# Delta layer: the outer products of the block solve run in pairs on two column tiles, and half of one output projection moves between them

## What is computed

```python
x = _layernorm(x + _L0_attn_ref(...))
...
x = _layernorm(x + _L1_attn_ref(x, w_qkvz, w_ba, conv_w, dt_bias, A_log, norm_weight, w_out))
...
x = _layernorm(x + _L3_ffn_ref(...))
```

## Time and profile before

| | us |
|---|---|
| median of 3 runs | 2424.78 |
| lowest and highest run | 2412.61, 2426.64 |
| span of the profiled execution | 2424.5 |
| PE, DVE, ACT, POOL busy in it | 2112.7, 1856.6, 1477.2, 216.2 |
| the delta layer's rounds 1 to 13, first `upper` to first `upper` | 715.52 |

### The profile page before, as it was taken

One profiled execution on the slowest core, in us unless ns is written; L12 is line 12 of the kernel. 1 busy time (PEld: TensorE's weight loads), 2 busy tenths in 40 slices (PEclk: granted clock), 3 DMA queues, 4 the chain that ended last, 5 costly groups with the idle time before them and its releaser, 6 DMA issues. The chain is left out here.

```text
span 2424.5 us, 42274 instructions
## 1 busy us (share of the span) xinstructions
PE 2112.7 (87%) x16920; PEld 1596.5 (66%) x16920; DVE 1856.6 (77%) x3341; ACT 1477.2 (61%) x2466; POOL 216.2 (9%) x163
## 2 busy tenths in 40 slices
PE   7997447999999999999986589899999996888855
PEld 4666325777777777878774345788888873555633
DVE  4776667888989898889867834478888776678697
ACT  3664255667777777776736631577777775455365
POOL 0000100000100010101100042000000000100313
PEclk8998768999999999999988799999999996999977
DMA  3000012222222221222116355311010000200001
GB/s 159 2 1 12 13 34 53 72 83 57 64 56 66 56 64 54 62 74 80 36 49 212 129 143 176 115 32 57 23 27 6 5 18 1 81 2 1 16 1 35
DMA packets 164785, 135.14 MB, mean 56 GB/s; under 512 B 118512, under 2 KB 145776, under 8 KB 157936
## 3 DMA queue, kind: packets, MB, share of 16 engines
q1 hardware_dynamic: 160752, 126.02, 16.6%
q0 software_dynamic: 3840, 6.43, 1.4%
HBM read 106.42 MB, written 25.98 MB: 55 GB/s over the span
## 5 line engine op out<-in xcount | busy, mean ns | idle before, releaser
L1593 DVE SCALAR_TENSOR_TENSOR ctx_chan<-l1a_raw,l1a_cw,ctx_chan 128x1024 f32<-128x1024 f32 x192 | 232.0, 1279 | 3.5 <-issue 3.5
L1200 PE MATMUL banks<-x_chan,l1a_wp 128*128 128x512 f32 x512 | 225.2, 598 | 4.8 <-ACT l1a_vt L1488 4.8
L1200 PEld LDWEIGHTS banks<-x_chan,l1a_wp 128*128 128x128 f32 x512 | 98.0, 192 | 122.6 <-issue 116.7
L3166 PE MATMUL banks<-x_chan,more_weights_ahead 128*128 128x128 f32 x1024 | 123.6, 275 | 1.2 <-ACT l2a_kT L2693 1.2
L3166 PEld LDWEIGHTS banks<-x_chan,more_weights_ahead 128*128 128x128 f32 x1024 | 121.6, 192 | 3.9 <-ACT l2a_kT L2693 2.0
L1187 POOL TENSOR_TENSOR l1a_al<-l1a_aT,l1a_outer 128x1024 f32<-128x1024 f32 x32 | 75.0, 2364 | 483.2 <-DVE l1a_aT L1653 483.2
L1237 PE MATMUL banks<-l1a_wo,l1a_oT 128*128 128x256 f32 x512 | 117.7, 383 | 0.0
L2706 ACT ACTIVATE l2a_masked<-l2a_masked,l2a_rowmax 128x128 f32<-128x128 f32 x256 | 99.0, 392 | 28.9 <-DVE l2a_rowmax L2919 28.9
L3202 PE MATMUL banks<-l2a_wo,l2a_oT 128*128 128x256 f32 x512 | 114.5, 382 | 0.0
L1208 PE MATMUL banks<-l1a_wz,x_chan 128*128 128x256 f32 x512 | 113.4, 380 | 0.0
L3202 PEld LDWEIGHTS banks<-l2a_wo,l2a_oT 128*128 128x128 f32 x512 | 96.2, 190 | 14.3 <-issue 1.0
(11 more groups left out here) (648 smaller groups left out, 5644.1 us busy)
## 6 DMA issues: line engine op xcount, KB each, us to landing
l1a_sq<-l1a_norm_mem SPq DMA_DIRECT2D x16, 1024.0 KB, 4.7
ctx_tok<-l1a_rows_mem SPq DMA_DIRECT2D x16, 1024.0 KB, 8.1
l1f_wgu<-in_l1f_wgu_dram SPq DMA_DIRECT2D x4, 1408.0 KB, 11.4
moe_sums<-l1x_zero SPq DMA_DIRECT2D x2, 2176.0 KB, 18.3
ctx_chan<-in_ctxT_dram SPq DMA_DIRECT2D x2, 2048.0 KB, 13.8
l1a_wp<-in_l1a_wp_dram SPq DMA_DIRECT2D x8, 512.0 KB, 5.5
l1f_wgu<-moe_sums SPq DMA_DIRECT2D x8, 512.0 KB, 7.5
x_chan<-in_xT_dram SPq DMA_DIRECT2D x4, 512.0 KB, 5.2
```

Of the source, the lines that this page charges most:

```text
L1200: mm = MM(projected(i, u)[:, q * 512:(q + 1) * 512], wp[:, c, u * 128:(u + 1) * 128], g.xT[:, c, t0:t0 + 512], start=c == 0, stop=c == 1)
L1593: V.scalar_tensor_tensor(t, raw[:, u, :, j:j + S], cw[:, c, j:j + 1], t, ALU.mult, ALU.add).then_inc(s["conv_done" if step == 2 else "conv ...
L3166: mm = mm_(ps[:, 4 + q % 2, k * 128:(k + 1) * 128], wq[:, c, SHARE * q + k, :], g.xT[:, c, tile(i)], start=c == 0, stop=c == 1)
```

## The change

Four things change in the delta layer. The eight `upper` of quarters 0 and 1 alternate, and quarter 1's results go to partitions 64 to 127 of its bank (`upper_rows`); the last eight `lower` alternate too, and quarter 3's results go to partitions 0 to 63 (`lower_rows`). ACT's copies of these two quarters read one half of the partitions and write the other. The last `lower` wait once, for all four additions to `vt`. Of `previous_out(1)` batches 0 and 1 stay where the whole was, batch 2 goes behind the first `upper`, batch 3 ahead of the last `lower`, and `out` is signalled with batch 3. On DVE `add(i-1, 1)` moves behind the additions to `vt`.

```diff
+        def upper_rows(q):
+            return quarter(q)[64:128] if q == 1 else quarter(q)[0:64]
+        def lower_rows(q):
+            return quarter(q)[0:64] if q == 3 else quarter(q)[64:128]
...
-            def project_out(h):
-                for b in range(4):
+            def project_out(h, first=0, stop=4):
+                for b in range(first, stop):
...
-                mm.then_inc(s["out"], 1)
+                if stop == 4:
+                    mm.then_inc(s["out"], 1)
...
-            def solve(i):
+            def solve(i, between):
 
                 pe.wait_ge(s["xT2_out"], 2 * i + 1)
-                for q in range(2):
-                    for k in range(4):
-                        mm = upper(q, k)
-                    mm.then_inc(s["u_made"], 1)
+                for k in range(3):
+                    upper(0, k)
+                    upper(1, k)
+                upper(0, 3).then_inc(s["u_made"], 1)
+                upper(1, 3).then_inc(s["u_made"], 1)
+                between(2, 3)
                 pe.wait_ge(s["xT2_out"], 2 * i + 2)
...
-                for q in range(2, 4):
-                    pe.wait_ge(s["vr_made"], 4 * i + q + 1)
-                    for k in range(4):
-                        mm = lower(q, k)
-                    mm.then_inc(s["w_made"], 1)
+                between(3, 4)
+                pe.wait_ge(s["vr_made"], 4 * i + 4)
+                for k in range(3):
+                    lower(2, k)
+                    lower(3, k)
+                lower(2, 3).then_inc(s["w_made"], 1)
+                lower(3, 3).then_inc(s["w_made"], 1)
...
-                previous_out(1)
+                previous_out(1, 0, 2)
...
-                solve(i)
+                solve(i, lambda first, stop: previous_out(1, first, stop))
...
-                    A(lows(uw, q), quarter(q)[0:64], ACT.Copy).then_inc(s["u_out"], 1)
+                    A(lows(uw, q), upper_rows(q), ACT.Copy).then_inc(s["u_out"], 1)
...
-                    A(highs(uw, q), quarter(q)[64:128], ACT.Copy).then_inc(s["w_out"], 1)
+                    A(highs(uw, q), lower_rows(q), ACT.Copy).then_inc(s["w_out"], 1)
...
-                if i:
-                    add(i - 1, 1)
                 for q in range(4):
                     v.wait_ge(s["r_made"], 4 * i + q + 1)
                     V.tensor_tensor(highs(vt, q), quarter(q)[64:128], highs(vt, q), ALU.add).then_inc(s["vr_made"], 1)
+                if i:
+                    add(i - 1, 1)
```

More of the change, by code:

```diff
@@ L1260, in upper @@
                 slot = 4 * q + k
-                return MM(quarter(q)[0:64, k, :], xT2[0:64, slot, :], vt[0:64, slot, :], start=True, stop=True)
+                return MM(upper_rows(q)[:, k, :], xT2[0:64, slot, :], vt[0:64, slot, :], start=True, stop=True)
             def across(q, k):
@@ L1268, in lower @@
                 slot = 4 * q + k
-                return MM(quarter(q)[64:128, k, :], xT2[64:128, slot, :], vt[64:128, slot, :], start=True, stop=True)
-            def solve(i):
+                return MM(lower_rows(q)[:, k, :], xT2[64:128, slot, :], vt[64:128, slot, :], start=True, stop=True)
+            def solve(i, between):
                 pe.wait_ge(s["xT2_out"], 2 * i + 1)
-                for q in range(2):
-                    for k in range(4):
-                        mm = upper(q, k)
-                    mm.then_inc(s["u_made"], 1)
+                for k in range(3):
[4 more added lines that the diff above has]
+                between(2, 3)
                 pe.wait_ge(s["xT2_out"], 2 * i + 2)
@@ L1339, in round_, with previous_out @@
                     gate_project(i, h)
-                def previous_out(h):
+                def previous_out(h, first=0, stop=4):
                     if not i:
@@ L1346, in previous_out @@
                     pe.wait_ge(s["oT_out"], 2 * i - 1 + h)
-                    project_out(h)
+                    project_out(h, first, stop)
                 def next_sums():
```

## The result

The changed kernel takes 2427.24 us (median of 13 runs, 2422.4 to 2430.83) against 2420.86 us before (13 runs, 2412.4 to 2426.64). The ratio is 1.0028, 95% interval 1.0016 to 1.0041: +6.8 us, between +4 and +10. Measured once more beside other kernels it was 1.0040 (1.0026 to 1.0055), +9.7 us. The change costs a third of a per cent. In microseconds against the kernel before, a ratio is always taken times 2421 here. The two profiled executions differ by only 1.6 us as a whole (2426.1 against 2424.5), because the changed kernel's reached its first `upper` at 410.42 in place of 419.04; the same kernel profiled again reached it at 416.47.

What follows compares the result with a forecast made beforehand. PE is busy 99.6%, but DVE's chains leave it only two half-microsecond slacks a round. Rounds 1 to 14 add +7.6, round 0 +0.1, round 15 +1.3: +9.0 us, 2434 us, 8 in 10 within 2410 to 2450.

Steps and rivals of the forecast that it cites:

- The two slacks: DVE's chains leave PE only about 0.5 us before the key product and 0.5 us before the p1 product each round.
- K: A round's first key product, which waits for DVE's gate; predicted 1.06 us later than before.
- The sum from T: Times counted from T, a round's first `upper`: `across` 2.01, last addition to `vt` 6.64, key product 14.05 us.
- the switch: PE's change between 64x64 and 128x128 tiles around a moved batch; taken as 0.13 us each way.
- the filler: A batch of `project_out(1)` moved into a PE gap: batch 2 before `across`, batch 3 before last `lower`; 1.13 us each.
- K to the p1 product: Stretch from key product to the product with p1: DVE's chain gives 35.68 in place of 36.2 us, a 0.5 gain.
- The sum over the rounds: Each of rounds 1 to 14: -0.5 + 1.06 = +0.54 us, times 14 = +7.6.
- Rival B: PE's clock falls in new gaps before `sum_squares`; most rounds lose 2 to 5 us, about 2470; chance 0.10.
- Rival A: PE sets the round after all, its saving shows: 1.2 us a round, 2408, or 2399 with free switches; chance 0.15.
- C: Paired products serialise, both moved batches add to the chain, key product at +1.95 us: 2447; chance 0.07.
- D: The moved add is covered, key product only 0.24 us later: 2423; chance 0.13.
- The last round: Round 15: add and four statistics ahead of the gate +2.6 us, `vt` additions -0.5, p1 product -0.8: +1.3.

Runs made afterwards that it cites:

- Experiment 1: Changed kernel with only its pairing and cross-half copies: `previous_out(1)` whole again, add back ahead of the additions to `vt`; ratio 1.0007 to the kernel before, +1.7 us.
- Experiment 2: Kernel before with one edit, `add(i-1,1)` moved behind the four additions to `vt`; ratio 1.0051 to the kernel before, +12.3 us.
- experiment 4: Changed kernel with `weigh` (two DVE instructions) moved to GpSimd ahead of `scale_out`; ratio 1.0287 to the kernel before, +69 us.
- experiment 5: Changed kernel with `weigh` on GpSimd, which first waits for the second `xT2` product, away from the convolution; ratio 0.9959 to the kernel before, -9.9 us.
- Experiment 8: Changed kernel with `add(i-1,0)` cut to 8 of 256 columns in rounds 1 to 14; ratio 1.0026 to the kernel before, +6.3 us.
- experiment 7: Changed kernel with the pairing alone undone, both batches and the add left in their new places; ratio 1.0090 to the kernel before, +22 us.

## Why the prediction was right, point by point

*The forecast.* 2434 us on a median of 2424.78, +9; measured +6.8 and +9.7. With 13 runs the kernel before is at 2420.86, so that the forecast stands 7 us above the measured 2427.24, of which 4 are the base of three runs.

*The two slacks.* This was the step that decided, and it held. With one half-microsecond slack at K and one ahead of the p1 product, PE's 1.7 us a round had nowhere to go. Experiment 1 shows it bare: 0.77 and 0.79 us of new idle time on PE, and no product earlier. Experiment 2 shows the slack at K: an add of 1.2 us moved K by 0.58.

*The sum from T.* Expected and measured in a typical round: `across` 2.01 and 2.08; last addition to `vt` ended 6.64 and 6.75; output products 7.81 and 8.02; add 6.90 and 7.11; gate 12.82 and 12.79; K 14.05 and 14.15. What is off is the switch. From the paired `upper` to the filler are 1.02 us (690.34 to 691.36), 0.88 of passes and 0.14 of switch; from the second filler to the `lower` 1.06 (696.28 to 697.34), 0.86 and 0.20. I had 0.13 each way; the way back to small tiles costs more. The passes are taken over from other rows, so the switches are estimates, some 0.7 us a round for all four. The Trainium skill names a drain at each change of tiling mode (TensorEngine Tiling (Array Packing), Key Properties). The rows agree in sign. PE alone could have started K at T + 13.44 (experiments 4 and 5, two fillers), where I had 13.23. The 1.16 us at K come half from the add and half from the fillers: 0.58 for the add alone (experiment 2), 0.26 because the first filler with its switches holds `across` and so `vr3`, and 0.33 because the add waits for the second filler's batch.

*K to the p1 product.* 35.68 expected; ahead of rounds 2 to 14 it took 35.2 to 36.6 and once 37.72, mean 35.7. The size was right, the holder only half: I named DVE's chain to p1 and put the squares in brackets. Experiment 8 shows that it is the squares. Both hang on DVE's convolution, so the sum came out the same; whoever went on to shorten p1 alone would have gained nothing. The averages also hide a change of limit. Before, this stretch was 36.05 us in ten of 13 rounds, whatever the block wait (0.20 to 0.82 us): PE set it. Now it is 35.0 plus the block wait (35.23 with 0.21, 36.64 with 1.60), so every block wait counts in full.

*The sum over the rounds.* Rounds 1 to 13: 13 x 0.54 = 7.0 expected, 724.59 - 715.52 = 9.1 measured. From T to K the rounds grew by 15.5 in place of 13.8: 0.1 us more in each, two of these 13 with K later by another 0.3 and 0.4, less one stall of PE (0.4) that stood in the profile before. K to the p1 product fell by 6.6, as expected, but with 0.8 of a fall of the clock in it; the rest of that fall, another 0.8, came behind p1, where the profile before had a stall of 0.6.

*Rival B, the clock.* It did happen, but only in the one round of this profile with the longest wait. PE's timeline ahead of round 14, and the window over it:

```profile
1185.52 1.81 PE L1234 MATMUL banks<-l1a_sq,ones 128*32 128x512 f32 x8 [2.47 <-ACT l1a_sq L1461]
1187.27 2.90 PE L1252 MATMUL banks<-l1a_xT,l1a_p 64*64 64x64 f32 x64
```
```profile
1186.00:1190.00 4.00, 4.00 (x72) 2.73 (x64) 4.00 (x5) 2.06 (x3) 0.00 (x0) 0.61 0.00 0
```

After 2.47 us without work the granted clock of the next 4 us was 0.61, part of it at 1.2 GHz; sums and p1 product took 1.6 us more than in the other rounds. In round 6 a wait of 2.17 us (sums at 740.14) had no such effect, nor had the usual 1 us. I had feared most rounds for 2 to 5 us each; it was one in fourteen, for 1.6, in both profiles of the changed kernel. For its gaps, mostly about 1 us, the chance was too high; the danger itself was real and near. In experiment 4, with gaps of 4.0 to 4.3 us, every round lost about 2.0. The length of the gap alone does not decide: after 2.36 us the clock fell (the changed kernel again, experiment 7), after 2.42 in experiment 5 it stayed at 1.00. What does was not tested.

*Rival A* fell with experiments 1 and 2, *C* with the 1.09 us of the paired passes and experiment 7, *D* with the 7.8 us that K waits for the gate.

*The last round.* I had +2.6 us for add and statistics ahead of the gate. The gate came at T + 11.00, against 10.58: +0.4 only. ACT's timeline and DVE's:

```profile
1254.39 1.28 ACT L1571 ACT_TABLE_LOAD   x1
```
```profile
1253.41 1.41 DVE L147 BATCH_NORM_STATS2 ln_stats_buf<-x_tok 128x6 f32<-128x256 f32 x4
...
1255.93 0.20 DVE L1823 RECIPROCAL ln_rstd_buf<-ln_rstd_buf 128x8 f32<-128x8 f32 x1 [0.36 <-ACT ln_rstd_buf L1571]
```

Before, DVE waited 2.4 us there for a square root, of which 1.28 was ACT loading its table after its last copy. Now DVE's statistics run while ACT loads it. I had carried the whole chain over as if every link moved with the add. So the agreement of the total is in part luck: here I was 1.7 us too high (2.6 less 0.5 expected, 0.4 measured), and at K 0.1 too low in each of 14 rounds.

## What to carry to other kernels

Before a faster order on the busiest engine is built, write down what each of its waits would be if it were faster, round by round: here the engine was busy 99.6% of the time and had half a microsecond to give at two places. Filler work that covers one gap opens another where it was taken from, and what it feeds (here an addition on another engine) moves with it; that dependent move was half of the loss at K, the fillers' own delays the other half. With one filler and the add put back where VectorE is idle anyway the loss was gone (-1 us); with one filler and `weigh` taken out of VectorE's chain it became -14. Work handed to GpSimd must be placed by what VectorE runs beside it. And a mean over a round can average two limits: read single rounds before adding up slacks.

## What the runs showed of the hardware

VectorE's convolution steps, whose two tensor operands lie in SBUF, took 2.86 and 2.92 us where GpSimd multiplied beside them and 1.27 where it did not (a mean of 1542 ns against 1277); `normalise`, of the same form, took 2.77 in place of 2.35 us for two beside a GpSimd instruction. The additions to `vt`, which read one operand from PSUM, took 694 ns beside GpSimd's product (experiment 5) and without it (the changed kernel). It works both ways: GpSimd's product took 2754 ns beside the convolution and 1902 beside additions out of PSUM. The Trainium skill says this (GPSIMD Engine Reference, Specifications): GpSimd's SBUF interfaces are shared with VectorE, with contention for DVE instructions with two SBUF inputs. The rows agree. The page gives no size; here it was 3.2 us a round on the convolution, and, with the fall of the clock that the longer waits brought, 79 us of the kernel between two places for the same two instructions.

TensorE's granted clock fell from 1.00 to 0.61 and 0.63 of full speed over the 4 us behind idle times of 2.47 and 4.15 us (experiment 4: to between 0.50 and 0.60 over 4.1 us in every one of 14 rounds with idle times of 4.0 to 4.3), and stayed at 1.00 behind one of 2.42 us (experiment 5).

Two 64x64 products that share their 64 rows and go to different column halves ran at 0.11 us a pair of passes, also when one of them is the same line of code with another output half; copies on ScalarE from partitions 64 to 127 to 0 to 63 and back took 0.59 us like those within a half.
